# Decoder layer over 32 row tiles: DMA transposes in the feed-forward stage, and re-ordered engine lists

## What is computed

```python
x = _layernorm(x + attn(x, ...))          # 16 heads, rotary, causal over 256 rows -> here 64
x = _layernorm(x + xattn(x, ctx, ...))    # banded attention, 8 heads, gated by ctx
x = _layernorm(x + ffn(x, ...))
def ffn(x):                               # w_gate_up [2048, 256], w_proj [256, 1024], ternary
    gate, up = split(x @ wq_gu.T)
    h = silu(gate) * up                   # 1024 wide
    return rms_norm(h) @ wq_p.T
```

## Time and profile before

| | us |
|---|---|
| three runs | 969.29, 969.61, 966.85 |
| median | 969.29 |
| the profiled execution | 966.67 |
| its span, from first to last instruction | 964.9 |
| granted TensorE clock, mean share of full speed | 0.98 |

### The profile page before, as it was taken

How to read it: one execution, slowest core, us unless ns; L and a number is a source line. 1 busy time by engine, 2 the same in 40 slices (tenths; PEclk the granted TensorE clock), 3 DMA queues, 4 the chain that set the end, 5 groups by cost and what they waited for, 6 DMA issues and landing times.

```text
span 964.9 us, 26409 instructions
## 1 busy us (share of the span) xinstructions
PE 885.0 (92%) x10486; PEld 542.3 (56%) x10558; DVE 867.2 (90%) x1719; ACT 813.4 (84%) x1395; POOL 817.1 (85%) x1133
## 2 busy tenths in 40 slices
PE   4779888999999999999999999999999998988985
PEld 2344455556666566666666556666666665554553
DVE  5999988999999999999999999999999999888754
ACT  2655667899999999999999999999999998988886
POOL 4885879999999999999999999999999999655652
PEclk9899989999999999999999999999999999999999
DMA  7000001000000000000000000000000000000000
GB/s 249 23 12 13 25 7 35 19 19 19 13 19 19 25 24 25 7 24 24 18 25 24 24 24 24 24 8 24 24 19 24 24 19 19 13 13 19 18 13 22
DMA packets 24825, 24.72 MB, mean 26 GB/s; under 512 B 4992, under 2 KB 23680, under 8 KB 24704
## 3 DMA queue, kind: packets, MB, share of 16 engines
q1 hardware_dynamic: 24704, 23.05, 8.2%
HBM read 14.12 MB, written 4.19 MB: 19 GB/s over the span
## 4 chain that ended last, share of the span: by engine, by line
PE 61%; DVE 26%; ACT 5%; issue 4%; POOL 4%; DMA 0%; SPq 0%; POOLq 0%; DVEq 0%
PE ps L621 7%; PE ps L543 6%; PE ps L740 6%; DVE hsplit L2650 5%; PE ps L428 5%; DVE rowmax L2575 5%; PE ps L570 4%; PE ps L505 3%; PE ps L531 3%; PE ps L688 3%; PE ps L707 3%; PE ps L487 3%; PE ps L471 2%; PE ps L632 2%; DVE rot L2484 2%
## 5 line engine op out<-in xcount | busy, mean ns | idle before, releaser
L2575 DVE TENSOR_REDUCE rowmax<-ps 128x4 f32<-128x768 f32 x256 | 243.2, 950 | 20.4 <-PE ps L570 19.7
L1526 ACT ACTIVATE prob<-ps 128x768 f32<-128x768 f32 x256 | 207.2, 809 | 40.1 <-PE ps L601 39.6
L2043 POOL TENSOR_TENSOR hsum<-hsum,minus_half 128x32 f32<-128x32 f32 x32 | 175.4, 5481 | 5.5 <-DVE hsum L2495 5.2
L2080 POOL TENSOR_SCALAR_AFFINE_SELECT prob<-prob 128x256 f32<-128x256 f32 (+1 forms) x256 | 140.5, 549 | 33.0 <-ACT prob L1526 33.0
L2082 POOL TENSOR_SCALAR_AFFINE_SELECT prob<-prob 128x512 f32<-128x512 f32 (+1 forms) x256 | 146.2, 571 | 0.0
L1501 ACT ACTIVATE high<-ps,bx_col 128x512 f16<-128x512 f32 x128 | 95.0, 769 | 14.6 <-PE ps L543 12.8
L621 PE MATMUL ps<-prob,v_pad 128*32 128x192 f32 x2048 | 105.0, 334 | 0.3 <-POOL prob L2082 0.3
L570 PE MATMUL ps<-k_rows,q_rows 24*128 24x192 f16 x1024 | 86.9, 247 | 9.6 <-DVE rowmax L2575 4.8
L601 PE MATMUL ps<-q_rows,k_rows 25*128 25x192 f16 x1024 | 86.7, 247 | 1.4 <-ACT prob L1526 0.9
L543 PE MATMUL ps<-x,wx_qk 64*128 64x256 f32 x512 | 73.9, 407 | 5.7 <-DVE prob_a L2513 4.5
L1602 ACT ACTIVATE hT<-ps 128x1024 f16<-128x1024 f16 x64 | 65.3, 1021 | 7.2 <-PE ps L722 7.2
(11 more groups left out here) (159 smaller groups left out, 2359.8 us busy)
## 6 DMA issues: line engine op xcount, KB each, us to landing
v_swap<-v_own SPq DMA_DIRECT2D x64, 68.0 KB, 2.0
xin<-in_x SPq DMA_DIRECT2D x32, 128.0 KB, 2.1
enc<-in_ctx SPq DMA_DIRECT2D x32, 128.0 KB, 2.2
out<-yout SPq DMA_DIRECT2D x32, 128.0 KB, 2.1
prob<-in_w_guT SPq DMA_DIRECT2D x4, 512.0 KB, 7.6
prob<-in_w_projT SPq DMA_DIRECT2D x2, 512.0 KB, 9.9
q_rows<-in_Wkv SPq DMA_DIRECT2D x1, 512.0 KB, 4.0
wx_qk<-in_wx_qk SPq DMA_DIRECT2D x1, 512.0 KB, 4.7
```

The lines of the kernel that those rows point to most:

```text
L1526: copy(prob[:, 2 * c:2 * c + 2, :, :].rearrange("p u a b -> p u (a b)"), ps[:, STB:STB + 2, 0:2 * QW], ACT.Exp, scale=float(XD) ** -0.5).t ...
L2043: g.tensor_tensor(hsum[:, 1, :], hsum[:, 0, :], minus_half[:, :], ALU.pow).then_inc(S["head_pow3"], 1)
L2080: g.affine_select(out=lead, in_=lead, compare_op=ALU.is_ge, fill=0.0, base=BAND - 64 * kb, pattern=[[0, 4], [1, cut]], channel_multiplier=-1)
L2575: v.tensor_reduce(of_head[:, hq:hq + 2, 2 * ng:2 * ng + 2], ps[:, MXB:MXB + 2, 0:2 * QW].rearrange("p j (a b) -> p j a b", a=2), AX, ALU.m ...
```

## The change

Four things change at once.

1. The transposes of the feed-forward stage are DMA transposes, started by SP. `do_xT` moves `xsplit` to `xsplitT` (128 KB), `do_hT1` moves `hsplit` to `hT` (512 KB, both halves in one transfer). The helpers `xT_ps` and `hT_ps` of PE and `xT` and `hT` of ACT are gone, and so is the fp16 identity and its load.
2. `xsplitT` and `hT` have three buffers instead of one. `xsplit` and `hsplit` still have one.
3. PSUM banks are dealt out anew: `gate_ps`, `down_ps`, `qk_ps`, `maxT_ps` use bank 5, `up_ps` and `vproj_ps` bank 6, `z_ps` bank 1, `v_ps` bank 0, and so on.
4. All lists (start, step, end) of all five engines are in another order, with other waits.

```diff
@@ block.sync
+            def do_xT(t):
+                sp.dma_start_transpose(xsplitT[:, t.buf, :, :], xsplit[:, :, :].rearrange("p a b -> p (a b)")).then_inc(s_xT, 16)
+            def do_hT1(t):
+                sp.dma_start_transpose(hT[:, t.buf, :, :, :].rearrange("p a b c -> p (a b) c"), hsplit[:, :, :].rearrange("p a b -> p (a b)")).then_inc(s_hT, 16)
+            def put_hT1(t):
+                sp.wait_ge(S["h_lo1"], t.at(1, 1))
+                do_hT1(t)
@@ block.tensor
-            def do_xT_ps(t):
-                for i in range(4):
-                    last = tr(bank16(G5)[:, 128 * i:128 * i + 128], xsplit[:, i // 2, 128 * (i % 2):128 * (i % 2) + 128], ident16[:, :])
-            def do_hT_ps(t, c):
-                for i in range(8):
-                    last = tr(bank16((G5, MXB + 1)[c])[:, 128 * i:128 * i + 128], hsplit[:, c, 128 * i:128 * i + 128], ident16[:, :])
...
             def put_gate_ps(t, c):
                 if c == 0:
+                    pe.wait_ge(s_xT, t.at(16, 16))
+                    if t.has(2):
+                        pe.wait_ge(S["y3"], t.back(2).at(1, 1))
...
             def put_down_ps(t):
-                pe.wait_ge(S["hT1"], t.at(1, 1))
+                pe.wait_ge(s_hT, t.at(16, 16))
@@ block.scalar
-            def do_xT(t):
-                copy(xsplitT[:, :, :].rearrange("p a b -> p (a b)"), bank16(G5)[:, 0:512], ACT.Copy).then_inc(S["xT"], 1)
...
             def put_h_hi(t):
                 act.wait_ge(S["hid_pow"], t.at(1, 1))
+                if t.has(1):
+                    act.wait_ge(s_hT, t.back(1).at(16, 16))
                 do_h_hi(t)
-            def do_hT(t, c):
-                copy(hT[:, c, :, :].rearrange("p a b -> p (a b)"), bank16((G5, MXB + 1)[c]), ACT.Copy).then_inc(S[f"hT{c}"], 1)
```

More of the change, by code:

```diff
@@ L216, in build @@
         s_maxrow = [sem(f"s_maxrow{b}") for b in range(3)]
+        s_xT = sem("s_xT")
+        s_hT = sem("s_hT")
         s_vswap = [sem(f"s_vswap{b}") for b in range(3)]
[L218 to L224, removed]
+        names = """aT aT_ps attn centred ct_ps down_ps enc exp gate_ps0 gate_ps1 gated hT1 h_hi h_lo1 head_pow3 heads0 heads1 hf
+                   hf_ps hid0 hid1 hid_pow high0 high1 high2 high3 max maxT_ps max_hi maxrow mx o_ps ot0 ot1 out proj_ps2
+                   proj_ps3 pt0 pt1 pt_ps0 pt_ps1 qk qkT qkT_ps qk_ps qkn rotated rows0 rows1 rows2 rows3 s_exp s_max s_ps s_sub
+                   sel silu0 silu1 sqsum squared st tanh0 tanh1 tr_ps0 tr_ps1 up_ps0 up_ps1 v v_ps val variance vpad vproj_ps
+                   vswap wo_ps x1 x1_nb x2 x2_hi x2_lo x2_nb xT x_pow x_stats xbo xload xn xnT xnT_ps xn_nb y1 y1_pow y1_stats y2
+                   y2_pow y2_stats y3 y3_pow y3_stats yout yout_nb z_ps zr attn_c centred_c heads_c variance_c x_stats_c
+                   y1_stats_c y2_stats_c y3_stats_c rotated_c eps0 eps1 eps2 eps3 eps_hid"""
         S = {n: sem("c_" + n) for n in names.split()}
@@ L421, in put_xnT_ps @@
                 pe.wait_ge(S["xn"], t.at(1, 1))
+                if t.has(5):
+                    pe.wait_ge(S["max_hi"], t.back(5).at(1, 1))
                 do_xnT_ps(t)
@@ new lines, in _ @@
+            do_qk_ps(tile[5])
+            pe.wait_ge(S["max"], tile[1].at(8, 1))
+            do_mx(tile[1], 1)
+            pe.wait_ge(S["exp"], tile[0].at(8, 1))
+            do_st(tile[0], 1)
+            keep_warm(1)
+            pe.wait_ge(S["rows1"], tile[1].at(1, 1))
+            do_vproj_ps(tile[1])
+            pe.wait_ge(S["max"], tile[1].at(8, 2))
+            do_mx(tile[1], 2)
+            pe.wait_ge(S["vpad"], tile[1].at(1, 1))
+            do_pt_ps(tile[3], 0)
+            pe.wait_ge(S["exp"], tile[0].at(8, 2))
@@ new lines, in _ @@
+            do_st(tile[2], 1)
+            pe.wait_ge(S["max"], tile[3].at(8, 1))
+            do_z_ps(tile[0])
+            pe.wait_ge(S["zr"], tile[0].at(1, 1))
+            do_mx(tile[3], 1)
+            pe.wait_ge(S["rows3"], tile[3].at(1, 1))
+            do_pt_ps(tile[5], 1)
+            do_vproj_ps(tile[3])
+            pe.wait_ge(S["pt1"], tile[5].at(1, 1))
+            pe.wait_ge(S["gated"], tile[0].at(1, 1))
+            do_ct_ps(tile[0])
+            pe.wait_ge(S["exp"], tile[2].at(8, 2))
@@ new lines, in _ @@
+            do_st(tile[3], 2)
+            do_mx(tile[4], 2)
+            pe.wait_ge(S["vpad"], tile[4].at(1, 1))
+            do_pt_ps(tile[6], 0)
+            pe.wait_ge(S["pt1"], tile[6].at(1, 1))
+            pe.wait_ge(S["qkn"], tile[7].at(1, 1))
+            do_qkT_ps(tile[7])
+            pe.wait_ge(S["exp"], tile[3].at(8, 3))
+            do_st(tile[3], 3)
+            pe.wait_ge(S["max"], tile[4].at(8, 3))
+            do_mx(tile[4], 3)
+            pe.wait_ge(S["pt0"], tile[6].at(1, 1))
@@ L1390, in _ @@
             pe.wait_ge(S["max"], tile[5].at(8, 3))
             do_mx(tile[5], 3)
-            pe.wait_ge(S["sel"], tile[3].at(4, 4))
+            do_st(tile[4], 2)
+            pe.wait_ge(s_xT, tile[1].at(16, 16))
+            do_gate_ps(tile[1], 0)
+            pe.wait_ge(S["vpad"], tile[5].at(1, 1))
+            do_pt_ps(tile[7], 0)
+            pe.wait_ge(S["pt1"], tile[7].at(1, 1))
+            pe.wait_ge(S["gated"], tile[2].at(1, 1))
+            do_ct_ps(tile[2])
+            pe.wait_ge(S["max"], tile[5].at(8, 4))
@@ L1558, in put_x2 @@
             def put_x2(t):
[L1559 to L1560 removed]
+                act.wait_ge(S["x2_nb"], t.at(1, 1))
                 do_x2(t)
```

2775 lines of the change are left out of this document (1508 added, 1267 removed).

## The result

The changed kernel takes 976.1 us (median of 4 runs, 976.05 to 978.11), the kernel before 968.43 us beside it (4 runs, 966.85 to 969.61). The ratio is 1.0084, with a 95% interval of 1.0049 to 1.0119: 8 us slower, where 954.0 us and a gain were forecast. The profiled execution took 978.11 us, of which the span is 976.1; that of before took 966.67.

A forecast was written before the change was run, and what follows sets the result against it. PE, DVE, POOL and ACT were all taken to be within a microsecond or two of full in each period. From the profiled 966.67 us, 16.9 gained and 4.2 lost at the end gave 954.0 us, range 938 to 1000.

The forecast's parts named there:

- The ramp: Start of the kernel: no cost of its own; half the steady gain of 0.65 us for the eight periods at both edges.
- The period: Steady part, one tile: 26.91 us falls to 26.25, bounds 25.6 and 26.9; 16.9 us gained including the edges.
- an order that isn't perfect: Steady period: a little added to the midpoint of DVE's two floors, giving 26.25 us.
- the two ends: Steady period, DVE's floor: 26.45 us if all its short gaps stay, 25.7 if all vanish.
- The elastic term: Steady part, DVE's h_lo1: 2081 ns there, 1.28 us when POOL is idle; a neighbour can give or take up to 0.8 us.
- The end: Last tile: the whole 6 us transfer stands open where 1.8 us stood; 4.2 us more, bounds 2.2 and 8.1.
- The removed work: Whole span: PE's transposes and ACT's copies go; PE busy some 52 us less, ACT some 84 us less.
- Rival C: SP's queue, steady part: the transpose in flight holds maxrow back once past 7 us of cover; 984 to 1040 us, chance 0.20.
- Rival D: Steady part: DVE, ACT and POOL get slower while DMA writes across SBUF; 970 to 990 us, chance 0.02.
- Rival B: Steady part: PE's and ACT's relief finds no taker, period stays 26.9 us; 964 to 975 us, chance 0.18.
- 1309 ns for a block: DMA transposes: a page's figure speaking against the change; as a rate 26.2 us a tile, not used in the sum.
- 261 GB/s: DMA transposes: a page's rate, an estimated 2 us for 512 KB beside the fixed part; not used in the sum.

The follow-up runs named there:

- e2: The changed kernel with the load of tile 2's x issued on SP ahead of the six 512 KB weight transfers; 971.84 us, 1.0019 times the kernel before.
- e1: The kernel before with its own lists, only the feed-forward transposes made DMA transposes with three result buffers; 958.59 us, 0.9889 times the kernel before.
- e5: The changed kernel with one more ACT pass (Square) over hid in each tile; 984.47 us in its one execution.
- e6: The changed kernel with each 512 KB transpose issued twice, first into a scratch tile, every wait for both; 987.60 us in its one execution.
- e7: The changed kernel with the DMA transposes from tile 3 on replaced by plain 8 KB transfers; 972.83 us, 1.0029 times the kernel before.
- e10: The changed kernel with h_lo1 moved behind max 3 in DVE's steady list; 994.18 us in its one execution.
- e8: e1 with a new end: last two tiles' product transposed in halves, h_lo1 moved ahead of y3, useless matmuls in PE's waits; 957.78 us, 0.9890 times the kernel before.
- e9: e8 with useless matmuls in two more PE waits near the end; 954.26 us, 0.9836 times the kernel before.

## Why the prediction was wrong

Forecast: -16.9 + 4.2 = -12.7 us. Measured: +11.44. The 24.1 us between them, by the steps of the sum:

- **The ramp, 15.7 us: the step that failed.** The forecast took half the steady gain over the eight periods at the edges (2.6 us gained) and costed the ramp at nothing. It was 13.05 us lost, of which up to 3.8 may be the luck of the two executions (11.44 against 7.67 by the medians). The start lists show `x_stats` of tile 2 ahead of `centred` of tile 0, and tile 2's load behind the weights; the earlier trace rows had those transfers at 7.6 and 9.9 us. By the trace of before, tile 0 does not wait for tile 2's x. That wait was there to be found before the run: a moved step counts with what it waits for. e2 showed it and its price, 3.6 us at once and 5.4 to 8.25 at tile 9. What the other moved steps of the ramp cost stays open.
- **The period, 7.0 us.** 26.25 us was forecast, 26.58 came: 22 x 0.33. With the old lists and only the transposes changed the period was 26.30. So the reasoning from PE's and ACT's relief to a floor near DVE's and POOL's need was right, and what failed was the allowance for "an order that isn't perfect". The middle of the two ends, 26.45 and 25.7, is 26.08: the allowance was 0.17 us and came to 0.50, with the old lists to 0.22. The elastic term was named rightly and went the good way, `h_lo1` falling from 2081 to 1276 ns. But DVE's busy time stayed at 25.7 us a period, as small operations were stretched by 0.8 us together, this one for example, before and now (225 to 790 us):

```profile
L2468 DVE SCALAR_TENSOR_TENSOR nb<-mv,rstd 128x1 f32<-128x1 f32 x21 | 3.2, 152 | 0.0
```

```profile
L2627 DVE SCALAR_TENSOR_TENSOR nb<-mv,rstd 128x1 f32<-128x1 f32 x21 | 6.9, 328 | 0.0
```

- **The end, 1.5 us.** 4.2 forecast, 5.73 measured. The size of the transfer was taken too large (6 instead of 4.4 us), and two things were left out: PE's clock falls while it stands, 1.7 us on the last matmuls, and the tiles before the last pay as well, though the 4.4 us fit between two of them: they leave 9.5 and 8.4 us apart, not 7.8, with `down_ps` waiting for its transfer. `h_hi` did not wait for it: that of the last tile starts at 960.55 us, 1.5 us after the transfer before it had landed, and was released by POOL.
- **The removed work.** The groups of the earlier trace rows are gone, but busy time fell by less than the forecast 84 us on ACT (62.5) and 52 on PE (5.9 here, 37.8 in e1): the sum of single durations counts twice where neighbours overlap in the records, and in the changed kernel PE runs at a lower clock in the ramp and at the end. How much of the difference is either was not measured. e5 shows that of ACT's share at least 1.05 us a tile has no taker.
- **Rival C** did not occur. The transpose was in before `maxrow` was issued, and e6 and e7 show that doubling it or taking it away moves the period by 0.03 us at most. **Rival D** neither: without the writes, in e7, DVE is busy 546.00 of 565 us, with them 546.08.
- **Rival B** named the mechanism that hurt (a new order sets the engines against each other otherwise) but put it into the steady part alone and let it cost the whole gain there; half the steady gain survived.
- The figure of the Trainium skill's page "VectorE: DVE Perf Modes", section The three transpose paths, 1309 ns for a block, isn't a rate: 16 blocks landed in 4.4 us, 0.28 us a block, and a second row of 16 behind it added 2.5 us, 0.16 us a block. The 261 GB/s of the Trainium skill's page "DMA: Bandwidth & Descriptors", section Latency and other measured facts, make an estimate of 2 us for 512 KB, close to these 2.5 us.

As for the chances: 0.26 was given to slower, 0.20 of it to a transfer that would hold back the queue. None stood for the one part of the change that was plain to read, lists ordered anew at the start. That the measured 976.1 us lies inside the range of 938 to 1000 is luck: above 975 that range was there for rivals C and D, which did not occur.

## What to carry to other kernels

When a change comes with new lists, read the start and the end of each list as closely as the repeated step, and ask of every step that moved what it waits for and what is queued ahead of that. Where the mechanism and the reordering come in one edit, try the mechanism with the old order first: here the one was worth 11 us, and the other, lists and banks together, cost 19. And a transfer that is free in a steady loop is paid for in full at the end, where splitting it, one swap and keeping PE busy in the waits brought all of it back.

## What the runs showed of the hardware

- A DMA transpose from SBUF to SBUF of 512 KB landed after 4.4 us and one of 128 KB after 2.4 us; two of 512 KB in a row needed 6.9 us. The issue of the large one held SP's queue for 2.06 us in the row shown, against 0.6 for a plain transfer.
- DVE and POOL exclude each other on some operations: which of the two started first decided whether `qkn` took 1.06 or 1.98 us and `h_lo1` 1.28 or 1.81. The Trainium skill's page "SBUF — State Buffer", section Who interferes with whom, says that a DVE instruction with two SBUF inputs contends with a GpSimd instruction that reads SBUF, and that the shared port pair is an exclusive lock; the swap in e10 agrees. It also says that DMA doesn't contend with the engines, and e7 agrees.
- In the ramp the granted clock from 110 to 140 us was 1.00, 0.85 and 0.74 in three executions with the same ramp code (e1, e8, e9), and tile 9 came at 220.85, 223.37 and 229.15 us. The three ran on three chips, but one chip scatters as much: e9's five executions lie between 950.39 and 959.11 us. That spread is as large as most effects studied here; only the cut by pieces keeps them apart.
- After 6.46 us without work 16 matmuls took 3.60 instead of 1.92 us, at a granted clock of 0.50, and matmuls without use in the wait kept them at 1.92. In e10's steady part the clock fell behind a wait of 1.0 us in six of 22 periods and not in the others, though PE had the same list of work in each.
